# Mixer B of a Mamba-style block: the squares summed by VectorE, and the first exponent unit cut in two inside the output product

## The reference

```python
proj = layernorm(x) @ in_proj_w * mup                 # z, xBC, dt
xBC = silu(causal_conv(xBC, conv_w, taps=4) + conv_b) # x (1024), B (128), C (128)
dt = softplus(dt + dt_bias); A = -exp(A_log)
def step(state, inp):                                 # over the tokens
    state = state * exp(dt_t * A) + dt_t * x_t (outer) B_t
    y_t = C_t . state
y = y + D * x
var = mean(square(y), axis=-1)                        # over all 1024 channels
out = y * rsqrt(var + EPS) * norm_w * silu(z)
x = x + out @ out_proj_w
```

## Time and profile before

| | |
|---|---|
| time, median of 3 runs | 2748.89 us (2747.4 to 2749.82) |
| the profiled execution | 2749.61 us, span 2747.9 us |
| TensorE busy | 2633.6 us, 96% of the span, 17644 matmul records |
| VectorE busy | 1938.2 us, 71% |
| ScalarE busy | 1430.7 us, 52% |
| GpSimd busy | 816.1 us, 30% |

### The profile page before, as it was taken

The page is one execution under the profiler, slowest core; times in us unless marked ns, Lnnn a source line. Parts: engine busy times, 40 slices in busy tenths (PEclk is TensorE's granted clock), DMA queues, the critical chain, the costliest instruction groups (busy, mean ns, idle before and its releaser), DMA issues. The chain is left out here.

```text
span 2747.9 us, 50333 instructions
## 1 busy us (share of the span) xinstructions
PE 2633.6 (96%) x17644; PEld 1824.1 (66%) x17644; DVE 1938.2 (71%) x3797; ACT 1430.7 (52%) x2450; POOL 816.1 (30%) x606
## 2 busy tenths in 40 slices
PE   8999999999999998999899999999999999997998
PEld 7777777777777775456676666766677666774454
DVE  5666666666666665397787777877777777876377
ACT  4444444445444543342566666656666666664342
POOL 2222222233332323143222333223222233222143
PEclk8999999999999999999999999999999999998999
DMA  4000000000000005245000000000000000003433
GB/s 130 23 24 23 23 23 23 23 23 23 23 27 31 19 16 212 102 158 208 13 24 23 23 23 15 23 23 23 8 23 23 23 23 15 16 17 135 160 128 138
DMA packets 79994, 139.57 MB, mean 51 GB/s; under 512 B 17958, under 2 KB 17958, under 8 KB 78892
## 3 DMA queue, kind: packets, MB, share of 16 engines
q1 hardware_dynamic: 70812, 125.92, 13.2%
q10 hardware_dynamic: 9104, 12.63, 1.3%
HBM read 104.98 MB, written 33.55 MB: 50 GB/s over the span
## 5 line engine op out<-in xcount | busy, mean ns | idle before, releaser
L746 PE MATMUL work<-b_xnT,shared_w 128*128 128x256 f32 x2304 | 528.8, 384 | 3.8 <-DVE b_parts L1429 2.2
L746 PE MATMUL work<-a_xnT,shared_w 128*128 128x256 f32 x2176 | 501.0, 387 | 1.3
L746 PEld LDWEIGHTS work<-b_xnT,shared_w 128*128 128x128 f32 x2304 | 427.6, 190 | 66.6 <-DVE b_parts L1429 4.0
L746 PEld LDWEIGHTS work<-a_xnT,shared_w 128*128 128x128 f32 x2176 | 413.1, 193 | 71.3 <-issue 12.3
L1478 DVE TENSOR_TENSOR b_decay<-b_decay,b_gt 128x768 f32<-128x768 f32 x256 | 265.3, 1068 | 75.8 <-ACT b_decay L1103 75.1
L1097 ACT ACTIVATE b_decay<-seg 128x768 f32<-128x768 f32 x256 | 197.1, 810 | 232.2 <-PE seg L916 226.9
L863 PE MATMUL work<-a_w_out,a_yz 128*128 128x512 f32 x512 | 233.7, 606 | 11.8 <-DVE a_y L1467 11.8
L863 PE MATMUL work<-b_w_out,b_yz 128*128 128x512 f32 x512 | 236.3, 606 | 6.9 <-DVE b_y L1467 6.9
L1342 DVE SCALAR_TENSOR_TENSOR shared_cv<-shared_pre,b_conv_w,shared_cv 128x256 f32<-128x256 f32 x480 | 214.5, 481 | 33.7 <-ACT shared_cv L1033 26.3
L1039 ACT COPY shared_z<-work 128x256 f32<-128x256 f32 (+1 forms) x192 | 84.5, 440 | 291.3 <-PE work L746 291.3
L1342 DVE SCALAR_TENSOR_TENSOR shared_cv<-shared_pre,a_conv_w,shared_cv 128x256 f32<-128x256 f32 x432 | 189.7, 482 | 63.2 <-ACT shared_cv L1033 57.5
(11 more groups left out here) (338 smaller groups left out, 4634.4 us busy)
## 6 DMA issues: line engine op xcount, KB each, us to landing
x_mid<-mixer_x_res SPq DMA_DIRECT2D x64, 256.0 KB, 2.0
shared_x<-in_L_attn_a_x SPq DMA_DIRECT2D x16, 512.0 KB, 3.5
mixer_x_res<-in_L_attn_a_x SPq DMA_DIRECT2D x32, 256.0 KB, 2.6
shared_w<-in_L_ffn_d_w SPq DMA_DIRECT2D x2, 4096.0 KB, 14.3
f_d_w<-in_L_ffn_d_w SPq DMA_DIRECT2D x2, 4096.0 KB, 15.7
f_x_res<-x_mid SPq DMA_DIRECT2D x8, 1024.0 KB, 5.7
shared_x<-x_mid SPq DMA_DIRECT2D x16, 512.0 KB, 3.9
mixer_x_res<-x_mid SPq DMA_DIRECT2D x32, 256.0 KB, 2.6
```

The costliest lines, as they stand in the source:

```text
L746: mm = nc.tensor.matmul(dst, w_in[:, k, col:col + m], xnT[:, k, :], start=(k == 0), stop=(k == KD - 1))
```

## The change

- The steps rs0 and prs of mixer B are gone, with the constant `quad_row`. In their place VectorE sums the eight blocks of squares itself (`add_squares`, a tensor_reduce from SBUF), as mixer A already does; at the head it stands behind `masked_gt`, and `make_xdt` of tile 0 moves behind `rms_var` (mixer B).
- In the middle of mixer B, `add_squares` and `from_state` of tile 1 come before the convolution of blocks 6 and 7, which was ahead of both. Block 8 moves behind the masks of slots 2 and 3.
- rt0 is a step of its own ahead of out0, in both mixers.
- seg0.0 at the head of mixer B is cut into two: the half over the banks of tile 0's x behind the third matmul of pout, the half over tile 1's behind the seventh. Each waits only for its own tile's `xt` and `xdt`. ScalarE takes the second bound behind the root and the first copy of xnT.

```diff
@@ head and schedule (TensorE's order)
-                    + (["prs"] if prev and not FOLD else []) + ["yoff0a", "yoff0b"]
+                    + ["yoff0a", "yoff0b"]
...
-                steps += ["rs0", "yoff1a", "yoff1b", "seg1.0", "rt0", "out0"]
+                steps += ["yoff1a", "yoff1b", "seg1.0", "rt0", "out0"]
@@ use
-                    elif name in ("rs0", "prs"):
-
-                        pe.wait_ge(sq_done, FREE + 2 * (2 * i + (name == "rs0")))
-                        for b in range(KE):
-                            q = b % 4
-                            mm = nc.tensor.matmul(bank[32 * q:32 * q + 32, 0:P], ones[:, 0:32], sq[:, b, :],
-                                                  start=(b < 4), stop=(b >= 4))
...
-                        column = ones[:, 0:1] if FOLD else c["quad_row"][:]
-                        mm = nc.tensor.matmul(bank[:, 0:1], rs[:], column, start=True, stop=True)
+                        mm = nc.tensor.matmul(bank[:, 0:1], rs[:], ones[:, 0:1], start=True, stop=True)
...
-                            if k == KE // 4 and name == "out0":
-                                use("rt0", sec)
-                            if k == KE // 2 and name == "pout" and PAIRED and n_tiles(i):
-                                seg_unit(2 * i, 0, i)
+                            if k in (KE // 2 - 1, KE - 1) and name == "pout" and PAIRED and n_tiles(i):
+                                seg_unit(2 * i, 0, i, (k // (KE // 2),))
@@ seg_unit
-                def seg_unit(tile, p, xt_last=None):
+                def seg_unit(tile, p, xt_last=None, slots=(0, 1)):
...
-                        pe.wait_ge(xt_ready, FREE + 4 * xt_last + 4)
+                        last = slots[-1] + 1
+                        pe.wait_ge(xt_ready, FREE + 4 * xt_last + 2 * last)
                         if PAIRED:
-                            pe.wait_ge(xdt_done, FREE + 2 * xt_last + 2)
+                            pe.wait_ge(xdt_done, FREE + 2 * xt_last + last)
...
-                            for k in range(4):
+                            for k in range(2 * slots[0], 2 * slots[-1] + 2):
@@ supertile of ScalarE
                     slot_bound(sec, 0, 0)
-                    slot_bound(sec, 0, 1)
+                    if not PAIRED:
+                        slot_bound(sec, 0, 1)
                     slot_exp(sec, 0, 0)
                     if prev:
                         out_rsqrt(2 * i - 1)
                     if nxt:
                         xnT_copy(sec, 0)
+                    if PAIRED:
+                        slot_bound(sec, 0, 1)
                     slot_exp(sec, 0, 1)
@@ supertile of VectorE, the head
                     masked_gt(sec)
-                    make_xdt(sec, 0)
                     if prev and not FOLD:
-                        square_sums(sec, "prs")
+                        add_squares(2 * i - 1)
+                    if not PAIRED:
+                        make_xdt(sec, 0)
                     from_state(sec, 0)
                     if prev:
                         rms_var(sec, "prt")
+                    if PAIRED:
+                        make_xdt(sec, 0)
                     make_xdt(sec, 1)
@@ supertile of VectorE, the middle
                         gate(sec, 0, (1,))
+                        add_squares(2 * i)
+                        from_state(sec, 1)
                         if nxt:
                             conv_blocks(sec, (6, 7))
-                        square_sums(sec, "rs0")
-                        from_state(sec, 1)
                         rms_var(sec, "rt0")
...
                             keep_column(sec)
-                            conv_blocks(sec, (8,))
                         slot_mult(sec, 1, 2)
                         slot_mult(sec, 1, 3)
+                        if nxt:
+                            conv_blocks(sec, (8,))
```

More of the change, by code:

```diff
@@ L259, in build_constants @@
     c["keep"] = sb("keep", [P, NSUP + 1])
-    c["quad_row"] = sb("quad_row", [P, 1])
     hd = sb("hd", [P, 2, 4, 16])
@@ L336, in _ @@
                                     ).then_inc(built, 1)
-            nc.vector.tensor_reduce(c["quad_row"][:], c["ident"][:].rearrange("p (q e) -> p e q", e=32)[:, 0:1, :],
-                                    mybir.AxisListType.X, ALU.add).then_inc(built, 1)
-            dve.wait_ge(built, 4)
+            dve.wait_ge(built, 3)
             nc.vector.tensor_scalar(c["sign_row"][:], c["low_row"][:], -2.0, 1.0, ALU.mult, ALU.add).then_inc(built, 1)
             nc.vector.tensor_scalar(c["s_row"][:], c["l_row"][:], -1.0, 1.0, ALU.mult, ALU.add).then_inc(built, 1)
-            dve.wait_ge(built, 6)
-            count = [6]
+            dve.wait_ge(built, 5)
+            count = [5]
             def link(ins):
@@ L579, in mixer_phase @@
         pro_steps = ["xnT0", "xnT1", "dt"] + blocks + ["z0a", "z0b", "z1", "z2", "sums", "small0"]
-        epi_steps = ["prt", "pout"] if FOLD else ["prs", "prt", "pout"]
+        epi_steps = ["prt", "pout"]
         first_uses, loop_uses, last_uses = ([s for s in schedule(*a) if is_use(s)]
@@ L654, in freed @@
                 eng.wait_ge(state_ready, FREE + i * 4 + 2 * int(name[5]) + (2 if FOLD else "ab".index(name[6]) + 1))
-            elif name in ("rs0", "prs"):
-                eng.wait_ge(rs_ready, FREE + i * 2 + (name == "rs0"))
             elif name in ("rt0", "prt"):
@@ L974, in run @@
                         elif is_use(name):
-                            if name != "rt0":
-                                use(name, sec)
+                            use(name, sec)
                         elif name[:5] == "ident":
@@ L984, in run @@
                             if kind[:3] == "seg":
-                                seg_unit(2 * sec.i + j, int(s), sec.i if (j, s) == (0, "0") else None)
+                                if s == "0a":
+                                    seg_unit(2 * sec.i, 0, sec.i, (0,))
+                                else:
+                                    seg_unit(2 * sec.i + j, int(s), sec.i if (j, s) == (0, "0") else None)
                             else:
@@ L1505, in gate @@
                                                 zs[:, cols, j * P:(j + 1) * P], ALU.mult).then_inc(yz_done, 1)
-                def square_sums(sec, name):
-                    dve.wait_ge(work_full, sec.full(name))
-                    nc.vector.tensor_copy(rs[:], sec.bank(name)[:, 0:P]).then_inc(rs_ready, 1)
                 def add_squares(tile):
@@ L1704, in _ @@
                 sec = epilogue()
-                if FOLD:
-                    add_squares(2 * NSUP - 1)
-                else:
-                    square_sums(sec, "prs")
+                add_squares(2 * NSUP - 1)
                 rms_var(sec, "prt")
```

1 line of the change is left out of this document (removed).

## The result

The kernel after takes 2753.53 us (median of 14 runs, 2750.94 to 2755.9), the kernel before, run on the same chips, 2748.07 us (14 runs, 2746.76 to 2749.86). The ratio is 1.0019, with a 95% interval of 1.0011 to 1.0027: slower, by 5.5 us. The forecast was 2761 us with a range of 2728 to 2773. The direction and the range hold; the size is less than half of the 12 us that were forecast.

The account below looks back on a forecast made before the run. TensorE was taken to bound the kernel. Middles +21.0, last middle -0.8, heads -6.0, mixer A -3.2 and epilogue +0.5 made +11.5 us on 2749.6, an execution 0.7 above the median: forecast 2761 us, range 2728 to 2773.

Parts of the forecast that it names:

- a supertile's middle is 1.4 us longer: Mixer B's middle: VectorE 5.5 us late, less 1.75, 0.9 and 1.45 swallowed; 15 x 1.4 = +21.0 us.
- The chain through the middle: Mixer B: convolutions take turns with GpSimd (8.3 us), rms_var 5.5 late, state_add 1.4 late, TensorE waits before sums.
- the convolutions don't wait: Rival, mixer B's middle: convolutions not delayed by GpSimd, middle gains 0.78 us; 2728 us, chance 0.18.
- VectorE keeps its turn: Rival, mixer B's middle: they contend, but VectorE keeps its turn or GpSimd comes late; 2730 to 2742 us, chance 0.10.
- partly: Rival, mixer B's middle: delay 4.5 us, middle gains or loses up to 0.4; 2743 to 2754 us, chance 0.10.
- main case: The forecast itself, with turns in the middle and a gain at the head: 2755 to 2767 us, chance 0.45.
- The new wait: Sign, mixer B's middle: TensorE waits about 1.5 us before the sums product, released by b_state.
- The head: Head of mixer B's supertiles: 0.4 us gained in 15 heads, each half unit 0.39 us, small1's wait 0.8 us.
- the head gives nothing: Rival, mixer B's head: second half, bound and exponent come later, no gain; 2767 or 2773 us, chance 0.17.
- Mixer A and rt0: Ahead of out0, rt0 costs nothing and saves 0.2 us; mixer A gains 16 x 0.2 = 3.2 us.
- The last supertile and what lies behind it: End of mixer B: last middle -0.8 us, having no convolutions; epilogue +0.5; -0.7 in the comparison of pieces.

Follow-up runs that it names:

- conv_first: From after, convolution of blocks 6 and 7 put back ahead of add_squares and from_state in mixer B's middle; 2728.68 us, 0.9929 of before.
- conv_late: From before, only the convolution of blocks 6 and 7 moved behind from_state of tile 1; 2772.08 us, 1.0082 of before.
- pool_waits: From after, GpSimd's three operations in mixer B's middle held until VectorE is through convolving blocks 6 and 7; 2728.17 us, 0.9925 of before.
- first_head: From after, mixer B's first supertile gets back the old order of make_xdt and of the bounds; 2748.92 us, 1.0003 of before.

## Where the prediction was right, and which step failed

**The step that failed is the term "a supertile's middle is 1.4 us longer", the remainder of 5.5 us that VectorE was to be late less the 4.1 us that it was to swallow.** Measured it is 0.79 us: VectorE is 4.9 us late and swallows 4.1. The term stands 15 times in the sum, so this is the larger part of the miss. The second step is a term put at nothing without a reason: the head of mixer B's first supertile, which costs 3.8 us. The mechanism itself, and with it the direction, was right.

- **The chain through the middle is as forecast.** The convolutions take turns with GpSimd; rms_var comes late; VectorE swallows most of it; the rest shows as a new wait at the sums product. conv_first and conv_late show that the place of the convolutions sets it off, pool_waits that GpSimd beside them is what makes them long and TensorE wait. The rivals in which the convolutions don't wait, or VectorE keeps its turn, are out. The rule of the Trainium skill (SBUF — State Buffer, "Who interferes with whom"), that two SBUF inputs contend with GpSimd and that whoever starts first blocks the other for its whole length, agrees with the row of 8.04 us and the single ones of 2.04 to 2.59; that tensor_reduce never contends, by the head of after, where it and a GpSimd operation lie side by side for 0.6 us and both last what they last elsewhere:

```profile
2014.93 1.93 DVE L1500 TENSOR_REDUCE b_rs<-b_sq 128x128 f32<-128x1024 f32 x1
```

```profile
2013.63 1.93 POOL L1759 TENSOR_TENSOR b_skip<-b_xt,b_d_skip 128x1024 f32<-128x1024 f32 x1 [0.71 <-ACT b_xt L1059]
```

- **Why 1.4 became 0.79.** The forecast has 0.6 us too much in each of 14 periods. rms_var stands at 1992.77 where 1993.4 was forecast, 4.9 us late and not 5.5. Of the 0.6, 0.25 are b_y, which is ready at 1984.80 and not at 1985.05, and 0.26 the six convolutions, 8.04 for 8.3: the turns were priced with 2.36, 1.92 and 1.93 less 0.2 each, which was too much by 0.1 a turn. Of what VectorE was to swallow, the masks gave 1.84 (forecast 1.75) and the waits about 2.3 (2.35). A residue of 1.4 between terms of 5.5 and 4.1 is a difference of large numbers: an error of a tenth in the one moved the result by half.
- **The rival "partly" has bounds that its own sum doesn't give.** With a middle longer by x the forecast's terms add up to 15x - 9.5 us, so a gain or a loss of 0.4 is 2734 to 2746 us, not 2743 to 2754; the measured 0.79 gives 2752. The measured 2753.5 lies outside the 2755 to 2767 of the forecast's main case and inside the stated bounds of "partly", but the delay of 4.9 us lies between the 4.5 of that rival and the 5.5 of the main case, and the loss is twice what the rival allows.
- **The new wait was named as 1.5 us and is 1.47, but that is no success.** By the sum it should have been 1.4 + 0.78 = 2.2, as TensorE arrives 0.78 earlier at the output product (0.68 earlier at the end of the state product: 0.79 + 0.68 = 1.47); the two places of the text don't fit each other.
- **The head is right:** 0.35 us gained (0.4), halves at 2021.94 and 2025.94, which in the forecast's count, where this supertile starts 0.79 us earlier, are 2021.15 and 2025.15 (21.3 and 25.2), a half for 0.38 us (0.39), small1's wait 0.73 (0.8). So the rival in which the head gives nothing is out. That a half costs as much as the whole is as the forecast has it: in the trace of before four matmuls of the unit, one for each group of rows, start within 0.01 us of each other and the other four 0.2 us behind; a half has two of each, over two groups. That 32-row tiles are independent, the Trainium skill says in TensorEngine Tiling (Array Packing) under "Key Properties", not under the heading that the forecast names; these rows agree.
- **Mixer A and rt0 are right in themselves** (0.22 us each, 0.2 forecast), and rt0 in mixer B too; the falls of the clock were no term of the sum, -3.4 in A and +3.4 in B. They cancel here by luck, and nothing in the forecast foresaw the 1.4 us that come with the clock at the very start.
- **The head of mixer B's first supertile was put at nothing.** The heads were counted as 15 because the first has no output product to overlap with; what the new order costs it was not asked. It costs 3.8 us in the period, by first_head against after. The period is 4.2 us longer than before's, the forecast had 1.4 for its middle alone, and what is left for that middle is 0.4.
- The last supertile and what lies behind it, forecast at -0.7, come to -1.3; this was not taken apart further, nor were the 0.4 us between mixer A's last supertile and mixer B.

So the miss of the sum, 11.5 against 3.8, is -7.8 for periods 2 to 15, +2.8 for the first period (+3.8 its head, -1.0 its middle), and -2.7 for all the rest (-1.8 ahead of mixer B, of which 1.4 the clock, -0.3 in A, -0.6 behind; the clock's four falls make 0).

## What to carry over

Before moving short VectorE instructions with two SBUF inputs, look at which of them will meet a long GpSimd operation: each one that does can stand blocked for most of a GpSimd operation (1.6 to 2.1 us here), so put few long ones there, or hold GpSimd for a moment, rather than many short ones. When a change gives its gain to one resource and its cost to the slack of another, price both more finely than the difference, since the small difference is multiplied by the number of iterations; and go through the first iteration by itself, where the work that covers the new order is missing. Two kernels are best compared by the periods of their steady part, with the falls of the clock counted apart.

## What the runs showed of the hardware

- VectorE's instructions with two SBUF inputs and GpSimd's take turns, one each: a queue of six of 0.48 us beside three of GpSimd takes 8.04 us, and 2.71 with GpSimd held back (pool_waits). With one of the inputs in PSUM there are no turns: the eight operations of the two xdt (`seg` times `b_dt`) lie beside GpSimd's three in the head of after and take 5.62 us, as two times 2.79 in the earlier trace rows.
- Matmuls over different groups of 32 rows run side by side in TensorE: eight small ones over four groups cost 0.39 us, and four of them over two groups, one slot's half, still 0.37 to 0.38, since each group has its two one after the other in either form.
- The granted clock fell to half for 3.4 us in single supertiles of the steady part, at the same matmuls in both profiles of before and of after; each fall costs 1.7 us. The falls of mixer A stand elsewhere or are gone with 0.22 us less in each of its periods.
